# Edge sums of a graph network: added blocks go in turn into two arrays of sums instead of one

## What is computed

```python
# relational layer: messages of an edge are rows of a table by (source, type), weighted
x = x + segment_sum(table[src, type] * edge_weight, dst)
# attention layer with 8 heads
out = segment_sum(attn[:, :, None] * Wh[src], dst)          # and the sum of attn itself, for the division
# continuous filter layer
agg = segment_sum(h[src] * W * C, dst)                       # W: a row of filters for each edge, C: a cutoff
```

## Time and profile before

| | us |
|---|---|
| median of 3 runs | 5543.76 |
| the profiled execution, first to last instruction (span) | 6173.2 |
| stage A, first gather to last add | 709.6 to 1335.5 |
| stage J, first gather to last add | 4082.6 to 4719.4 |
| stage M, first gather to last add | 5167.8 to 5789.9 |
| busy in the whole span: PE / DVE / ACT / POOL | 4074.4 / 3273.6 / 2796.0 / 3072.9 |
| L607, the gathers of a stage, each | 0.946 median, 416 in a stage |
| L775, the adds of a stage, each | 0.422 to 0.430 median, 416 in a stage |

### The profile page before, as it was taken

How to read it: one execution, slowest core, us unless ns; L and a number is a source line. 1 busy time by engine, 2 the same in 40 slices (tenths; PEclk the granted TensorE clock), 3 DMA queues, 4 the chain that set the end, 5 groups by cost and what they waited for, 6 DMA issues and landing times. The chain is left out here.

```text
span 6173.2 us, 66416 instructions
## 1 busy us (share of the span) xinstructions
PE 4074.4 (66%) x17366; PEld 2897.1 (47%) x17366; DVE 3273.6 (53%) x7095; ACT 2796.0 (45%) x6254; POOL 3072.9 (50%) x3130
## 2 busy tenths in 40 slices
PE   7888555567837777256485776857776774555665
PEld 4555333347824445222264444835555662223465
DVE  6444355456555566699634665255556125444532
ACT  4777333322335566466343442335553213666532
POOL 3666566633446566267414552436662323666333
PEclk8999777768957887699796887967776886777888
DMA  4444533355643333355502223543333324566356
GB/s 129 150 150 148 114 90 91 90 124 180 174 115 91 94 96 95 72 167 166 135 1 61 47 43 104 179 118 95 95 95 70 118 63 129 179 181 181 81 159 203
DMA packets 442553, 721.00 MB, mean 117 GB/s; under 512 B 150695, under 2 KB 322521, under 8 KB 437660
## 3 DMA queue, kind: packets, MB, share of 16 engines
q1 hardware_dynamic: 299057, 374.14, 21.6%
q0 software_dynamic: 139600, 337.72, 20.1%
q10 hardware_dynamic: 3530, 4.89, 0.2%
HBM read 565.71 MB, written 153.73 MB: 117 GB/s over the span
## 5 line engine op out<-in xcount | busy, mean ns | idle before, releaser
L631 PE MATMUL ps<-msg,same 128*125 128x256 f32 (+1 forms) x2496 | 953.6, 524 | 671.2 <-issue 269.6
L631 PEld LDWEIGHTS ps<-msg,same 128*125 128x125 f32 x2496 | 566.1, 251 | 986.6 <-issue 574.2
L888 POOL DMA_INDIRECT msg<-d_gat,src_i x416 | 406.0, 976 | 266.9 <-PE ps L949 137.8
L253 POOL DMA_INDIRECT rec<-rec,slot_i x391 | 379.7, 971 | 304.4 <-DVE rec L431 133.6
L607 POOL DMA_INDIRECT msg<-d_lin,src_i x416 | 393.2, 945 | 275.0 <-issue 101.9
L607 POOL DMA_INDIRECT msg<-rel_rows,src_rel x416 | 399.0, 959 | 223.1 <-issue 95.4
L607 POOL DMA_INDIRECT msg<-d_gat,src_i x416 | 393.5, 946 | 226.3 <-PE ps L631 90.7
L949 PE MATMUL ps<-msg,same 128*125 128x260 f32 x832 | 300.5, 495 | 175.9 <-DVE agg_c L1111 130.9
L278 PE MATMUL ps_f<-w,hs 128*128 128x256 f32 x1568 | 383.6, 398 | 48.9 <-DVE rec L431 30.4
L278 PEld LDWEIGHTS ps_f<-w,hs 128*128 128x128 f32 x1568 | 298.8, 196 | 156.9 <-issue 61.3
L2962 PE MATMUL ps_y<-pr,ident 128*128 128x447 f32 (+1 forms) x448 | 209.3, 593 | 238.3 <-DVE pr L3044 238.3
(11 more groups left out here) (632 smaller groups left out, 9885.5 us busy)
## 6 DMA issues: line engine op xcount, KB each, us to landing
w<-in_L_ffn_packed SPq DMA_DIRECT2D x170, 514.0 KB
fil<-rec SPq DMA_DIRECT2D x104, 512.0 KB
rows<-bc_d SPq DMA_DIRECT2D x96, 447.0 KB
rel_rows<-row SPq DMA_DIRECT2D x25, 896.0 KB
got<-answered SPq DMA_DIRECT2D x30, 560.0 KB
ahead<-in_L_ffn_packed SPq DMA_DIRECT2D x8, 2052.0 KB
lo_rows<-ffn_lo_r SPq DMA_DIRECT2D x32, 500.0 KB
msg<-d_gat,src_i POOLq DMA_INDIRECT x832
```

The source lines that it names most:

```text
L253: nc.gpsimd.indirect_dma_start(k.rec, bass.IndirectOffsetOnAxis(slot_i[0:some_rows, c:c + 1], 0), rec[0:some_rows, g % R, j, :], None).the ...
L631: nc.tensor.matmul(ps[:, j, 0:width], same[:, g % 2, j, :], msg[:, g % R, j, 0:width], start=True, stop=True).then_inc(mm, 1)
L888: nc.gpsimd.indirect_dma_start(msg[:, g % R, j, :], None, table, bass.IndirectOffsetOnAxis(idx[:, n:n + 1], 0)).then_inc(msg_in[g % R], 16)
```

## The change

Each of the three stages has a second array of sums, `odd`, of the same size as the tiles' rows (125 partitions, 25 tiles, 256 or 264 numbers). Blocks 0 and 2 of a group are added into `acc`, blocks 1 and 3 into `odd`. Two adds in a row never touch the same array, and an add waits only for the one before the last. `odd` is cleared at the start of the stage, and after the last block it is added to `acc` as a whole. Nothing else is different: no instruction of PE, ACT, POOL or the DMA queues is added, removed or moved.

```diff
         ps = s.ps("ps", [P, G, 512])
+        odd = s.sb("odd", [P, NT, width])
...
                     for j, t in enumerate(tiles):
                         n = g * G + j
                         dve.wait_ge(mm, n + 1)
-                        if n:
-                            dve.wait_ge(added, n)
-                        into = acc[:, ds(t, 1), :].rearrange("p t f -> p (t f)")
+                        if n >= 2:
+                            dve.wait_ge(added, n - 1)
+                        into = (odd if j % 2 else acc)[:, ds(t, 1), :].rearrange("p t f -> p (t f)")
                         nc.vector.tensor_tensor(into, into, ps[:, j, 0:width], ALU.add).then_inc(added, 1)
 
                 if first:
                     c = Chain(dve, chain)
+                    nc.vector.memset(odd[:], 0.0).then_inc(zeroed, 1)
+                    dve.wait_ge(zeroed, 1)
                     learn(0, c)
...
                     nc.vector.tensor_tensor(k.key[:], k.key[:], ps_n[:, 0:NT], ALU.add)
+                    dve.wait_ge(added, BLK)
+                    nc.vector.tensor_tensor(acc[:], acc[:], odd[:], ALU.add)
                     return
+                nc.vector.memset(odd[:], 0.0).then_inc(zeroed, 1)
                 nc.vector.memset(acc[:], 0.0).then_inc(zeroed, 1)
-                dve.wait_ge(zeroed, 1)
+                dve.wait_ge(zeroed, 2)
...
                 sums(NGB - 1)
+                dve.wait_ge(added, BLK)
+                nc.vector.tensor_tensor(acc[:], acc[:], odd[:], ALU.add)
```

## The result

The changed kernel took **5565.74 us** (median of 20 runs, 5555.88 to 5573.38), the kernel before, timed beside it, 5540.4 us (20 runs, 5532.95 to 5559.8). The ratio is 1.004 with a 95% interval of 1.0033 to 1.0048: 18 to 27 us slower, and inside the half per cent that counts as the same. The forecast was 5562 us.

The account below looks back on a forecast made before the run. POOL's gathers, 5.0 us a group of four, were taken to bind the kernel. Final adds +21.3, A's memset +1.0 and the tail -3.7 gave +18.6 us on 5543.8, so 5562 us, range 5510 to 5585.

Parts of the forecast that it names:

- The pauses are recording, POOL binds: All stages: PE's pauses mostly the cost of recording; in runs that count POOL sets 5.0 us a group.
- the rival of the full ring: Stages A and J: PE's pauses real, POOL waits for the ring, faster adds count; 5407 up to about 5515 us, chance 0.15.
- The adds' distance, 0.63 to 0.34 us: DVE's adds within a group: without the wait 0.34 us apart, each wait worth 0.29 us, 0.87 us a group.
- The end of the range at which nothing is gained: DVE's adds: stay 0.63 us apart if run-time address computation takes up the time; 5566 us, chance 0.10.
- the exception that the prediction named: DVE's adds: the skill's rule of waiting for an empty pipe has an exception for a semaphore that is not held.
- The tail, -1.2 us a stage: Adds of the last two groups, behind the last gather: 0.87 and 0.36 us saved, -3.7 us for three stages.
- The final adds, +21.3 us: Stage ends: three exposed whole-array adds, 6.83 + 6.83 + 7.04 us, plus 0.63 us for the waits ahead.
- The memset of A, +1.0 us: Start of A, ahead of `learn(0)`: ends about when the edge list lands or little later; between nothing and 5.5 us.
- a sign of being right: Start of A in the changed profile: the first gather comes at most 1 us later.
- The memsets of J and M, nothing: Start of J and M: first scaling 5.5 us later, covered before POOL's 25th gather, so no cost.
- slower beside a denser DVE: POOL's gathers: becoming slower beside denser DVE work was one explanation listed for a median over 5572 us.
- The profile's span: Profile of the changed kernel: 60 to 140 us less span was expected.

Follow-up runs that it names:

- Experiment 1: The kernel before, unchanged, profiled once more: 5536.47 us.
- experiments 4 and 5: Only blocks 0 and 2 of each group gathered, `msg` cleared once: 5158.41 us in the kernel before, 5017.43 us in the changed kernel.
- experiment 6: The changed kernel with stage A's memset of `odd` moved behind `learn(0)` and the first weights: 5573.9 us, ratio 1.0058.
- experiment 7: The changed kernel with A's memset behind the first weights, DVE waiting for line 746 before it and for the memset after it: 5566.07 us (one run).

## Why the prediction was right, point by point

- **The pauses are recording, POOL binds.** Right in what the forecast needs, and it carried the forecast: the pauses do not belong to the kernel. That recording makes them is still inferred from their rhythm, since the one execution that had them was not timed without it. Experiment 1 shows the same program without them, experiments 4 and 5 show DVE's pace once POOL is relieved: 3.98 us a group in J, the very figure of the prediction, and differences of 0.80, 0.75 and 0.01 us a group where the rival of the full ring had put 0.87, 0.65 and none. That rival's arithmetic was sound, its premise false.
- **The adds' distance, 0.63 to 0.34 us.** Right in J, 0.34, and in M, 0.33. In A the prediction did not see that PE holds most adds, at 0.43 or 0.85 us; only with half of the gathers are they 0.33 us apart there. The end of the range at which nothing is gained, and with it what the Trainium skill says ("VectorE: DVE Perf Modes", The DRAIN you can't avoid: eight copies take 13.88 us with or without a semaphore after each), does not hold for these adds. The measurement decides: with the wait 0.63 us, without it 0.34. That is on the side of the exception that the prediction named.
- **The tail, -1.2 us a stage.** This is the term that was mis-sized. From the last gather to the last add were 12.42, 15.08 and 13.85 us in experiment 1, and 12.45, 14.77 and 13.53 after: nothing in A and 0.3 us each in J and M, 0.6 in place of 3.7. (Single profiles differ by as much: in the second one of the change J's were 13.87.) The step took 0.51 us of PE for a block, from a stretch at the higher clock, and gave the group before the last its full 0.87 us. In the trace PE is what the adds wait for in the last group, in A in the last three, at 0.85 to 0.88 us a block. The granted clock there was 0.56 of full speed in J's last 7 us, near the lower of TensorE's two levels (1.2 of 2.4 GHz), after 4.3 us in which PE had nothing to do.
- **The final adds, +21.3 us.** Right: 20.69. The three waits ahead of them were put at 0.21 us each and cost next to nothing: the last add of J ends at 4208.24 + 0.43 = 4208.67, the final one starts at 4208.70.
- **The memset of A, +1.0 us.** Nearly right: 9.81 us from load to gather against 8.49 in experiment 1, +1.3, a little over the 1 us that the prediction gave as a sign of being right.
- **The memsets of J and M, nothing.** Right: their gathers take 519 us with them and without.
- **Left out:** some 2.5 us that A's gathers lose with the relaxed waits. The prediction named a gather "slower beside a denser DVE" only as a sign of being wrong; it happened, in a small size.
- **The profile's span.** For the profile of the changed kernel the prediction still expected the pauses, and 60 to 140 us less than 6173. It was 609 us less, since they did not come at all.

The sum of what was seen: 20.7 + 1.3 + 2.5 - 0.6 = 23.9 us, against 25.3 from the medians and 18 to 27 by the interval. The forecast's 18.6 was 3.1 short in the tail, 2.5 in A's gathers and 0.3 in the memset, and 0.6 over in the final adds: 5.3 us in all. The predicted time came closer than the predicted difference by luck: 5562 us misses 5565.74 by 4 us, but it starts from a median of three runs that is 3.4 us over the later 5540.4, and the difference misses by 6.7.

## What to carry to other kernels

Before reading any wait in a profile, hold its span against the timed median: where it is some per cent longer, as 6173 against 5544 us here, find out what recurs with the count of recorded instructions, or take the profile again. A wait on an engine that idles for a slower one in each group costs nothing, and its removal shows only when the slower engine is relieved; half of the gathers turned the same edit from +25 into -141 us. An edit with a fixed cost outside the pipeline, like the final add of two arrays, needs a gain that lies on the path, so count the path's time first.

## What the runs showed of the hardware that was not expected

A gather's issue on POOL can be held by DVE. It took 7.34 us in place of 0.95 when a 5.39 us memset stood without waits between DVE instructions of which some have two SBUF inputs (experiment 6). With a wait ahead of the memset and one behind it the gathers took 0.95 (experiment 7), and beside the same memset in M 0.96. In the small, gathers that start together with such an instruction of 0.26 us took 1.08 to 1.10 us. The Trainium skill ("GPSIMD Engine Reference", 1. Specifications) lists GpSimd's SBUF interfaces as shared with VectorE, with contention from instructions in a 2-port performance mode or with two SBUF inputs. The longer gathers beside line 746 agree with that, at 1.08 to 1.10 us for 0.95. A hold that lasts through a memset, which has no SBUF input at all, is what experiment 6 adds; which of its neighbours makes it last is open.

The same program was profiled at 6173.2 and at 5534.7 us. The medians of the kernel before, wherever several runs of it were timed, were 5540 to 5544 us, so the long profile shows something that its timed runs do not have.
